# A piecewise-linear GELU on TensorE: sixteen short kinks sent once in place of fourteen sent in two parts

## What is computed

```
def float2fix(x, bits):            # round to multiples of 2^-bits
    s = 2.0 ** bits
    return round(x * s) / s

def pwlin_gelu_basic(x, bits_in, bits_out):
    xq = float2fix(x, bits_in)
    y = interp(xq, PWL_X, PWL_Y)   # 33 points of the exact GELU on [-4, 4]
    y = where(xq > 4.0, xq, where(xq < -4.0, 0.0, y))
    return float2fix(y, bits_out)

h = layernorm(x) @ w1 + b1         # 1024 -> 512
h = float2fix(h, 8)
h = pwlin_gelu_basic(h, 8, 8)
out = float2fix(h @ w2 + b2, 8)    # 512 -> 1024
x = x + out
```

## Time and profile before

| | us |
|---|---|
| median of 3 runs | 3458.6 |
| lowest and highest | 3450.61, 3459.63 |
| profiled execution | 3460.86 |
| its span, first to last instruction | 3459.1 |
| mean granted clock of TensorE | 0.972 |

### The profile page before, as it was taken

The page is one execution under the profiler, slowest core; times in us unless marked ns, Lnnn a source line. Parts: engine busy times, 40 slices in busy tenths (PEclk is TensorE's granted clock), DMA queues, the critical chain, the costliest instruction groups (busy, mean ns, idle before and its releaser), DMA issues. The chain is left out here.

```text
span 3459.1 us, 43729 instructions
## 1 busy us (share of the span) xinstructions
PE 3192.6 (92%) x14812; PEld 2595.8 (75%) x14812; DVE 2705.0 (78%) x4736; ACT 1129.0 (33%) x1445; POOL 1015.0 (29%) x698
## 2 busy tenths in 40 slices
PE   6899999978999998998689999998999996899998
PEld 5678888857888886776568888887788885677776
DVE  5577777757777776558699999998999875788886
ACT  2011111121111111123245555555555443445444
POOL 1256777757767667720000000000000000000000
PEclk8999999999999999999899999999999998999999
DMA  7943333343444444445588878887788765222221
GB/s 260 363 81 66 54 70 55 61 125 75 95 86 91 85 95 114 94 107 154 151 211 222 228 214 219 218 218 213 213 220 218 185 165 151 69 89 71 71 89 42
DMA packets 332845, 484.90 MB, mean 140 GB/s; under 512 B 199146, under 2 KB 199246, under 8 KB 332726
## 3 DMA queue, kind: packets, MB, share of 16 engines
q1 hardware_dynamic: 142644, 401.03, 40.8%
q0 software_dynamic: 184656, 65.68, 11.0%
q10 hardware_dynamic: 5426, 16.70, 1.3%
HBM read 391.39 MB, written 90.80 MB: 139 GB/s over the span
## 5 line engine op out<-in xcount | busy, mean ns | idle before, releaser
L1357 PE MATMUL G_acc<-values,whole_plain 125*125 125x257 f32 x5000 | 1117.5, 385 | 82.6 <-DVE whole_plain L1317 67.4
L1357 PEld LDWEIGHTS G_acc<-values,whole_plain 125*125 125x125 f32 x5000 | 944.0, 190 | 246.2 <-DVE whole_plain L1317 80.1
L330 POOL DMA_INDIRECT counts<-E_twins_now,E_cells_now x400 | 874.3, 2186 | 378.5 <-issue 247.6
L1252 ACT ACTIVATE whole_plain<-whole_plain,G_asrc_slope 125x750 f32<-125x750 f32 (+1 forms) x400 | 375.9, 944 | 335.0 <-DVE whole_plain L1308 333.2
L1308 DVE SCALAR_TENSOR_TENSOR whole_plain<-whole_plain,G_asrc_most 125x750 f32<-125x750 f32 (+1 forms) x400 | 412.3, 1031 | 59.0 <-PE G_acc L1357 42.3
L1317 DVE SCALAR_TENSOR_TENSOR whole_plain<-whole_plain 125x750 f32<-125x750 f32 (+1 forms) x400 | 388.4, 971 | 49.6 <-ACT whole_plain L1252 49.5
L952 DVE SCALAR_TENSOR_TENSOR N_least<-xT_plain,asrc_all,N_least 125x750 f32<-125x750 bf16 (+1 forms) x336 | 340.3, 1018 | 0.0
L1226 POOL DMA_DIRECT2D gat<-xT_plain x100 | 53.4, 535 | 972.4 <-ACT xT_plain L1268 972.4
L227 PE MATMUL V_v_ps<-whole,xT_space 128*125 128x512 f32 x1200 | 293.3, 402 | 35.2 <-DVE xT_space L255 24.1
L227 PEld LDWEIGHTS V_v_ps<-whole,xT_space 128*125 128x125 f32 x1200 | 221.3, 187 | 106.9 <-DVE xT_space L255 42.5
L227 PE MATMUL Q_q_ps<-whole,xT_space 128*125 128x512 f32 x1200 | 288.2, 399 | 13.9 <-DVE xT_space L255 13.9
(11 more groups left out here) (173 smaller groups left out, 3384.1 us busy)
## 6 DMA issues: line engine op xcount, KB each, us to landing
whole_plain<-counts SPq DMA_DIRECT2D x450, 328.1 KB
whole_plain<-counts SPq DMA_DIRECT2D x150, 382.8 KB
counts<-K_zeros POOLq DMA_DIRECT2D x50, 763.5 KB, 9.0
xT_whole<-xnT SPq DMA_DIRECT2D x75, 500.0 KB, 3.6
whole_plain<-counts SPq DMA_DIRECT2D x450, 38.1 KB
xnT<-xT_whole SPq DMA_DIRECT2D x25, 500.0 KB, 7.9
gat<-xT_plain POOLq DMA_DIRECT2D x100, 125.0 KB, 4.1
E_row<-edge_keys ACTq DMA_DIRECT2D x25, 488.3 KB
```

Source lines behind the costliest of these rows:

```text
L330: nc.gpsimd.indirect_dma_start(out=counts_cells, out_offset=bass.IndirectOffsetOnAxis(ap=self.cells_now[:, slot, c:c + 1], axis=0), in_=se ...
L1252: nc.scalar.activation(here, here, ACT.Exp, bias=asrc_slope[:, u % H, j:j + 1]).then_inc(exp_ready, 1)
L1357: m = nc.tensor.matmul(acc[0:T, t, 0:CW], weight[:, k % RING, t * T:(t + 1) * T], values[:, j, u % H, :], start=(j == 0), stop=(j == NT - 1))
```

## The change

The even function becomes the part of GELU that is left when max(h, 0) is taken off it (`BENT`), and it is again a sum of 16 kinks of |h|. The kinks' weights are rounded to eleven bits one after the other, each taking up the error of those before it (`short_kinks`); an assertion says that the rounded curve is the same at all 1025 sizes that |h| can have. So a weight needs no low part. TensorE gets all sixteen terms, each sent once. ScalarE makes terms 1 to 15. VectorE's `second_half` is gone, and the join adds max(h, 0) in place of half of `halves`. Ahead of the tiles, the kinks' low part on VectorE is gone as well.

```diff
+BENT = [y - 0.5 * x for x, y in zip(KNOTS, EVEN)]
+BITS = 11
+def short(x):
+    unit = 2.0 ** (math.frexp(x)[1] - BITS)
+    return round(x / unit) * unit
+def short_kinks():
+    kinks, at, slope = [], 0.0, 0.0
+    for below, above in zip(BENT, BENT[1:]):
+        kinks.append(short(4.0 * (above - at) - slope))
+        slope += kinks[-1]
+        at += 0.25 * slope
+    return kinks
+SHORT = short_kinks()
...
-    KN, PE_TERMS = len(KINKS), 14
-    kinks = sb("kinks", [T, 2, KN, T], F32R)
+    KN = len(SHORT)
+    kinks = sb("kinks", [T, KN, T], F32R)
...
-    terms = sb("terms", [T, PE_TERMS, F], F32R)
-    folded = sb("folded", [T, KN - PE_TERMS, F])
+    terms = sb("terms", [T, KN, F], F32R)
...
-    BY_SCALAR = range(1, PE_TERMS)
+    BY_SCALAR = range(1, KN)
...
-            high(nc, kinks[:, 0, :, :], kinks_whole).then_inc(kinks_high, 1)
+            high(nc, kinks[:, :, :], kinks_whole).then_inc(kinks_ready, 1)
...
-            def second_half():
-                chain.step(nc.vector.tensor_scalar(halves[:, :], hid[:, :], -4.0, -4.0, ALU.max, ALU.add))
-                for n, i in enumerate(FOLDED):
-                    chain.step(nc.vector.tensor_scalar(folded[:, n, :], magnitude[:, :], -KNOTS[i], 0.0, ALU.add, ALU.max))
-                chain.settle()
-                chain.step(nc.vector.scalar_tensor_tensor(out=halves[:, :], in0=hid[:, :], scalar=4.0, in1=halves[:, :],
-                                                          op0=ALU.max, op1=ALU.add))
-                for n, i in enumerate(FOLDED):
-                    chain.settle()
-                    chain.step(nc.vector.scalar_tensor_tensor(out=halves[:, :], in0=folded[:, n, :], scalar=2 * KINKS[i],
-                                                              in1=halves[:, :], op0=ALU.mult, op1=ALU.add))
...
-            dve.wait_ge(kinks_high, 1)
-            low(nc, kinks[:, 1, :, :], kinks_whole, kinks[:, 0, :, :]).then_inc(kinks_ready, 1)
...
-                dve.wait_ge(even_done, g + 1)
-                chain.step(nc.vector.scalar_tensor_tensor(out=gelu[:, :], in0=halves[:, :], scalar=0.5, in1=even_ps[:, :],
-                                                          op0=ALU.mult, op1=ALU.add))
+                dve.wait_ge(bent_done, g + 1)
+                chain.step(nc.vector.scalar_tensor_tensor(out=gelu[:, :], in0=hid[:, :], scalar=0.0, in1=bent_ps[:, :],
+                                                          op0=ALU.max, op1=ALU.add))
...
-                if fixed(g, 0, NT - 2):
-                    second_half()
...
-                for i in range(PE_TERMS):
+                for i in range(KN):
                     if i == 0:
                         pe.wait_ge(first_term, g + 1)
                     else:
                         pe.wait_ge(terms_scalar, g * len(BY_SCALAR) + i)
-                    for s in range(2):
-                        last = nc.tensor.matmul(even_ps[:, :], kinks[:, s, i, :], terms[:, i, :],
-                                                start=(i == 0 and s == 0), stop=(i == PE_TERMS - 1 and s == 1))
-                last.then_inc(even_done, 1)
+                    last = nc.tensor.matmul(bent_ps[:, :], kinks[:, i, :], terms[:, i, :], start=(i == 0), stop=(i == KN - 1))
+                last.then_inc(bent_done, 1)
```

More of the change, by code:

```diff
@@ L53, with curve @@
 EVEN = [0.5 * x * math.erf(x / math.sqrt(2.0)) for x in KNOTS]
-KINKS = [4.0 * (EVEN[i + 1] - EVEN[i]) - (4.0 * (EVEN[i] - EVEN[i - 1]) if i else 0.0) for i in range(16)]
+BENT = [y - 0.5 * x for x, y in zip(KNOTS, EVEN)]
[10 more added lines that the diff above has]
+    return kinks
+def curve(size, kinks):
+    return sum(kink * max(size - knot, 0.0) for kink, knot in zip(kinks, KNOTS))
+KINKS = [4.0 * (BENT[i + 1] - BENT[i]) - (4.0 * (BENT[i] - BENT[i - 1]) if i else 0.0) for i in range(16)]
+SHORT = short_kinks()
+assert all(round(256.0 * curve(n / 256.0, KINKS)) == round(256.0 * curve(n / 256.0, SHORT)) for n in range(1025))
 assert NT * T == N and NCH * CH == E and UNITS * CPU == NCH and UNITS == 2 * NT and sum(GROUPS) == NT
@@ L1387, in feed_forward @@
     work = sb("work", [T, 4, F])
-    hid, magnitude, halves, gelu = (work[:, i, :] for i in range(4))
-    terms = sb("terms", [T, PE_TERMS, F], F32R)
-    folded = sb("folded", [T, KN - PE_TERMS, F])
+    hid, magnitude, gelu = (work[:, i, :] for i in range(3))
+    terms = sb("terms", [T, KN, F], F32R)
     geluT = sb("geluT", [128, 2, FB, T], F32R)
@@ L1394, in feed_forward @@
     tr, hid_ps = ps("tr", [128, KB, 128]), ps("hid_ps", [T, F])
-    even_ps, gelu_tr, fed_ps = ps("even_ps", [T, F]), ps("gelu_tr", [128, FB, 128]), ps("fed_ps", [128, D])
+    bent_ps, gelu_tr, fed_ps = ps("bent_ps", [T, F]), ps("gelu_tr", [128, FB, 128]), ps("fed_ps", [128, D])
     raw1 = a["whole_plain"][:, 0, 1, :, :]
@@ L1410, in feed_forward @@
     w_high, w_low, kinks_ready = [sem("w1_high"), sem("w2_high")], [sem("w1_low"), sem("w2_low")], sem("kinks_ready")
-    kinks_made, kinks_high = sem("kinks_made"), sem("kinks_high")
+    kinks_made = sem("kinks_made")
     def parts_of(raw):
@@ L1415, in parts_of @@
         return slice(0, k), slice(k, 2 * k)
-    BY_SCALAR = range(1, PE_TERMS)
-    FOLDED = range(PE_TERMS, KN)
+    BY_SCALAR = range(1, KN)
     TILES = dict(lead=1, step=RING, tail=2)
@@ L1558, in weights @@
                     low(nc, w[:, 1, part, :], raw[:, part, :], w[:, 0, part, :]).then_inc(w_low[i], 1)
-            for i, kink in enumerate(KINKS):
+            for i, kink in enumerate(SHORT):
                 chain.step(nc.vector.memset(kink_row[:, i:i + 1], kink))
@@ L1598, in body @@
                     split(g + 2)
-                if fixed(g, 0, NT - 2):
-                    second_half()
-            over_tiles(dve, body, chain=chain, steps=1 + LN_STEPS + 1 + 4 + 2 * len(FOLDED), **TILES)
+            over_tiles(dve, body, chain=chain, steps=1 + LN_STEPS + 1 + 2, **TILES)
             finish(NT - 1, NT - 1)
```

2 lines of the change are left out of this document (1 added, 1 removed).

## The result

| | median us | lowest to highest | against before |
|---|---|---|---|
| before | 3457.8 (5 runs) | 3450.6 to 3459.6 | |
| after | 3433.8 (5 runs) | 3430.2 to 3437.2 | 0.9936 (0.9921 to 0.9952) |

The account below looks back on a forecast made before the run. TensorE was taken to set the round, with ScalarE's fifteen terms setting it after the change; -25.2 (24 rounds) + 2 - 1.0 + 2 (first and last tile) = -22.2 us gave a median of 3436.4, range 3424 to 3448.

Parts of the forecast that it names:

- The hand-over: From ScalarE's last term to TensorE's hidden product: 0.38 us, between 0.28 and 0.61, read from the first tile of before.
- Fifteen terms: ScalarE's fifteen terms per tile take 9.32 us, ending after TensorE could be through its sixteen matmuls, at 7.92.
- Hidden product to terms: From the hidden product's start to ScalarE's first term: a chain of 9.08 us that the change leaves alone.
- The round: One steady tile: 9.08 + 9.32 + 0.38 = 18.78 us, 1.01 below 19.79; over 24 rounds 25.2 us less.
- VectorE at nothing: Dropping VectorE's second half costed at nothing: curve's result ready about 12 us after first term, some 3 us become waiting.
- TensorE's 12 matmuls: Curve on TensorE falls from 28 to 16 matmuls, 2.79 us per round; 1.78 of it turns into holes.
- The first tile's clock: First tile: TensorE's granted clock rises only once the hidden product runs; costs 2 us, between 0 and 5.6.
- The last tile: Curve's result taken 9.97 us after the first term, 1.0 less; last fed-forward product 2 us slower by the clock.
- The sum: Whole change: -25.2 + 2 (first tile) - 1.0 + 2 (last tile) = -22.2 us, a median of 3436.4.
- Rival 1: TensorE's own work stays the round's bound, which loses 2.79 us: 70 us less in all, 3389; chance 0.03.
- Rivals 3 and 4: Terms 0.65 apart or hand-over near 0.61, about 3449, chance 0.09; sending once needs two passes, 22 us slower, chance 0.01.
- Rival 2: Holes between the last curve matmuls lower TensorE's clock each round, 1.41 us each, 34 us in all: 3470; chance 0.06.

Follow-up runs that it names:

- half_kept: Changed kernel, but VectorE still runs the six instructions of the second half, into a tile nobody reads: 3431.7 us, ratio 0.9946.
- vector_3: Changed kernel, but VectorE makes terms 13 to 15 and ScalarE only 1 to 12: 3386.5 us, ratio 0.9805.
- warm: Changed kernel with extra TensorE matmuls into an unread bank, filling holes in the first and last tile only: 3429.8 us, ratio 0.9914.
- sent_twice: Changed kernel, but each of the sixteen terms is sent twice, with low parts that are zero: 3482.1 us, ratio 1.0060.
- thin_1: Changed kernel, but ScalarE makes the very last of its terms twice, first into a spare tile: 3478.6 us, ratio 1.0070.
- thin: Changed kernel, but ScalarE makes each of its last five terms twice, first into a spare tile: 3560.9 us (2 runs), ratio 1.0293.
- thin_2: Changed kernel, but ScalarE makes the last two of its terms twice, first into a spare tile: 3505.3 us (1 run).
- vector_1: Changed kernel, but VectorE makes term 15 and ScalarE 1 to 14: 3418.9 us, ratio 0.9904.

## Why the prediction was right

- **The hand-over**, taken as 0.38 between 0.28 and 0.61: 0.39 measured (3241.29 to 3241.68). The row of the first tile of before was enough.
- **Fifteen terms**, 9.32 forecast: 9.31. **Hidden product to terms**, 9.08: 9.06. **The round**, 18.78: 18.76. From the first tile's first term to the last's, 450.7 + 2 forecast: 3400.89 - 2948.65 = 452.2. In this term lies something that the prediction doesn't argue: before's 475.95 holds a second round of 21.21 us, 1.4 above the usual one, as its fed-forward product takes 7.29. (Ahead of it TensorE had waited 1.68 us for the curve's result on VectorE.) The 24 equal rounds take it for granted that the changed kernel doesn't pay this. It came so, there is no such wait in its first tile and its second round is 18.80, but the prediction gives no reason.
- **VectorE at nothing**: the result was forecast at about 12 us after the terms' start, it came at 11.8, and VectorE waits 3.7 us for the hidden sum where some 3 were expected. `half_kept` shows that the 3.3 us were slack once the rest of the change was in.
- **TensorE's 12 matmuls**: 2.79 us off its list, 1.03 realised; `vector_3` brings out the rest, so the size of the term was right too.
- **The first tile's clock**, taken as 2 between 0 and 5.6: 20.62 - 18.76 = 1.9. `warm` shows that it is the clock. The 2 was a choice between bounds, not a reading.
- **The last tile**: VectorE takes the curve's result 9.97 us after the terms' start, as forecast. The last product's price, taken as 2 by a row of 1.4, was 2.4. The size came out, but part of its reason, the thin curve, is not shown: `vector_3` and `sent_twice` pay it behind a curve without holes. That before, with the same two waits, did not pay it stays unexplained.
- **The sum**: -22.2 us forecast, -22.3 in the stage. By parts: the steady rounds 24 x 1.02 = 24.4 and before's long second round 1.4 on one side, 1.9 in the first tile and 1.4 behind the last first term on the other, 22.5 in all, which is 22.3 within the spread of the rounds. That it agrees to 0.1 us is luck; the terms at the two ends were each known to a few us.
- **Rival 1** (3389, TensorE's work stays the bound) did not happen, but it is what `vector_3` makes of the kernel, 3386.5. **Rivals 3 and 4** did not happen: terms stayed 0.61 apart, and one pace holds for all. `sent_twice` has the cost of rival 4, 22 us: its stage is 21.6 us above that of before.
- **Rival 2**, the holes take the clock, did not happen in the changed kernel, but 0.06 was given for a poor reason. The argument against it was one idle stretch of 2 us at full clock. `thin_1` shows that making one of the five holes 0.6 us longer does it in most rounds, at up to 1.55 us each, close to the 1.41 forecast for it. With the instruction's own length that turns a gain of 22 us into a loss of 23. That one stretch of idleness didn't take the clock in before says little about five holes in a row ahead of a product.

The Trainium skill's rule in TensorE: Matmul & The Clock Gate, section "A second HAM failure mode: psum-queue depth-cycling", was weighed in the prediction and set aside. The changed kernel's own rows don't show it (granted clock 1.00 over 443 us); those of `thin_1` agree with it (0.50 and back in most rounds). The section "Why this matters for your kernels" of the same page of the Trainium skill warns of long idle gaps between bursts of matmuls; in `thin_1` no hole of the curve is longer than about 1 us, so heeding that alone is not enough here.

What stays open: how the holes' place in the round decides whether the clock falls (no run moved them without lengthening them), and why the clock held in the last tile of before alone.

## What to carry to other kernels

When work is taken off the engine that sets the round, ask what each remaining producer can deliver in the new round: here the last of ScalarE's terms came 1.4 us after TensorE could have been through, and moving three cheap terms to the engine that had just been relieved was worth twice the change itself. Measure each half of a two-part edit alone; one half gave all of the gain here. Look at the first and the last tile by themselves too: their clock made up to 2.8 us there, and fills belong only where TensorE has time for them. And count it as a risk when a dense list of matmuls becomes one that waits term by term ahead of a long product: the next small delay may cost a clock level, not its own length.

## What the runs showed of the hardware that was not expected

- ScalarE's activations of 125x512 start 0.615 us apart, whether TensorE reads each at once or not: 13 take 8.09 us, 15 take 9.31, 14 give a round 0.62 shorter.
- With one 0.6 us instruction more per round, 17 of the 23 rounds of `thin_1` behind the first lost time to the granted clock, with five waits of at most 1.0 us for ScalarE in each curve.
- In `thin`, the rounds grew from 23.1 to 23.9 us over the first seven tiles and then stayed at 23.89 to within 0.01, while those of `thin_2` jump between 20.0 and 22.8. Why the ones settle and the others jump is not shown.
- In the changed kernel the clock did not rise in the first tile while TensorE, at 1.2 GHz, sent one matmul per 0.61 us; it did in before and in `warm`, with two, and in `vector_1`, where a late term of VectorE made it send the waiting ones without a hole.
- In the last tile the granted clock fell in six of the seven kernels without fills or doubled terms, around waits of 1.31 and 1.39 us with four transposes between them, whatever the curve ahead was like (14 to 32 matmuls, with holes or without).
